# Cross-attention with two branches on one core: another order of VectorE's and ScalarE's work inside a batch

## The reference

```python
query = x @ Wq;  keyt = enc @ Wk;  valt = enc @ Wv
hs = mha(query, keyt, valt)                      # 100 queries, 718 keys, 8 heads
ca_q1 = einsum('btc,th->bch', ca, Wq_ca)[:, picked_100_rows, :]
ca_hs1 = mha(ca_q1, x, x)                        # second branch, 100 keys
ca_hs2 = mha(ca_hs1 @ Wq, ca @ Wk_ca, ca @ Wv_ca)   # 4 keys
out = (hs + ca_hs2) @ Wout + b_out + x
```

## Time and profile before

| | |
|---|---|
| runs | 995.15 us median (993.74 to 997.84) |
| the profiled execution | 995.7 us, its span 994.0 us, mean granted clock 0.995 |
| PE matmuls | 968.8 us busy, 97% |
| DVE | 709.8 us, 71% |
| ACT | 491.7 us, 49% |
| POOL | 343.2 us, 35% |
| DMA | 195 MB, mean 196 GB/s |

### The profile page before, as it was taken

One profiled execution on the slowest core, in us unless ns is written; L12 is line 12 of the kernel. 1 busy time (PEld: TensorE's weight loads), 2 busy tenths in 40 slices (PEclk: granted clock), 3 DMA queues, 4 the chain that ended last, 5 costly groups with the idle time before them and its releaser, 6 DMA issues.

```text
span 994.0 us, 21024 instructions
## 1 busy us (share of the span) xinstructions
PE 968.8 (97%) x6644; PEld 945.5 (95%) x6644; DVE 709.8 (71%) x1257; ACT 491.7 (49%) x911; POOL 343.2 (35%) x302
## 2 busy tenths in 40 slices
PE   9999899999999999999999999999999999998998
PEld 8998789999999999999999999999999999997997
DVE  6455677777777778787777777777777777777444
ACT  6434545455554546464646363636464645454120
POOL 5222253434242516060615252433333433424000
PEclk9999999999999999999999999999999999999999
DMA  7899967797878797979797868787888878795364
GB/s 260 278 287 269 273 155 191 184 206 182 196 184 200 182 190 189 191 191 190 198 182 197 188 194 194 193 180 202 181 213 163 226 162 218 164 223 149 101 188 142
DMA packets 157545, 195.21 MB, mean 196 GB/s; under 512 B 81040, under 2 KB 111568, under 8 KB 157520
## 3 DMA queue, kind: packets, MB, share of 16 engines
q1 hardware_dynamic: 150000, 181.53, 74.7%
q10 hardware_dynamic: 7520, 13.35, 4.4%
HBM read 82.74 MB, written 19.95 MB: 103 GB/s over the span
## 4 chain that ended last, share of the span: by engine, by line
PE 83%; DVE 8%; issue 3%; ACT 2%; SPq 1%; DMA 1%; ACTq 0%; DVEq 0%
PE psS L780 21%; PE psB L815 16%; PE psB L820 8%; PE psS L755 7%; PE psT L796 6%; PE psS L930 6%; PE psT L848 4%; PE psT L854 2%; PE psB L827 2%; PE psB L825 2%; DVE negmax L1580 1%; DVE probs L1591 1%; PE psB L965 1%; PE psB L880 1%; PE psB L903 1%
## 5 line engine op out<-in xcount | busy, mean ns | idle before, releaser
L780 PE MATMUL psS<-encT_keep,Wk_keep 128*128 128x360 f32 x1440 | 255.7, 331 | 1.8 <-ACT probs L1172 1.8
L780 PEld LDWEIGHTS psS<-encT_keep,Wk_keep 128*128 128x128 f32 x1440 | 239.2, 189 | 2.8 <-issue 1.4
L1172 ACT ACTIVATE probs<-psS,negmax 100x718 f32<-100x718 f32 x128 | 110.2, 861 | 137.1 <-DVE negmax L1580 137.1
L815 PE MATMUL psB<-PT_h,encN_h 128*128 128x400 f32 x480 | 169.3, 353 | 0.0
L815 PE MATMUL psB<-PT_l,encN_h 128*128 128x400 f32 x480 | 165.6, 345 | 0.0
L635 POOL TENSOR_TENSOR encT_keep<-encT_raw,encT_keep 128x718 fp32r<-128x718 f32 x45 | 83.5, 1856 | 181.7 <-ACT encT_keep L1201 177.2
L1597 DVE TENSOR_TENSOR PT_l<-psT,PT_h 128x600 fp32r<-128x600 f32 x128 | 99.5, 778 | 39.5 <-ACT PT_h L1183 36.0
L626 POOL TENSOR_TENSOR Mbd<-Mbd,fmask 128x320 fp32r<-128x320 f32 x48 | 43.1, 898 | 219.4 <-DMA Mbd<-m_split 216.8
L1580 DVE TENSOR_REDUCE negmax<-psS 100x1 f32<-100x720 f32 x128 | 114.8, 897 | 0.0
L1591 DVE TENSOR_SCALAR probs<-probs,inv 100x718 f32<-100x718 f32 x128 | 108.8, 850 | 4.5
L1183 ACT ACTIVATE PT_h<-psT 128x600 fp32r<-128x600 f32 x128 | 85.7, 669 | 44.6 <-PE psT L796 40.9
(11 more groups left out here) (253 smaller groups left out, 1793.5 us busy)
## 6 DMA issues: line engine op xcount, KB each, us to landing
kstack<-kT SPq DMA_DIRECT2D x64, 448.8 KB
kstack<-kT SPq DMA_DIRECT2D x192, 112.2 KB
enc_raw<-in_encN_dram SPq DMA_DIRECT2D x48, 384.0 KB, 4.4
encT_raw<-in_encT_dram SPq DMA_DIRECT2D x45, 359.0 KB, 5.2
kstack<-kT SPq DMA_DIRECT2D x32, 359.0 KB
kstack<-kT SPq DMA_DIRECT2D x32, 269.2 KB
kstack<-kT SPq DMA_DIRECT2D x32, 179.5 KB, 3.4
kstack<-kT SPq DMA_DIRECT2D x64, 89.8 KB, 3.8
```

The costliest lines, as they stand in the source:

```text
L780: mm = pe.matmul(keys_in(f, first)[:, half, 0:HALF], w[:, c, f * 128:(f + 1) * 128], e[:, c, k0:k0 + HALF], start=(j == 0), stop=(j == 3 * ...
L815: pe.matmul(psB[:, 1, 0:RH], eN[0][:, k, cc], PT[p][:, k, rows], start=(k == 0 and p == 0), stop=False)
L1172: nc.scalar.activation(halves(P[h % PRING][0:S, 0:KEYS]), without_overlap(psS[score_slot[h]], S), ACT.Exp, bias=negmax[:, h:h + 1], accum_ ...
```

## The change

Nothing is computed otherwise; calls move within ACT's and DVE's lists.

In batches 1 to 15 on DVE, `u_low(i-1, 2)` goes ahead of `b2_norm`. In every batch `xm_low` goes ahead of `norm(i, 5)`, and `norm(i, 6)` goes from ahead of `keys`' low part `k_low(i+1, 0)` to behind `rowmax(i, 7)`. In batch 0 `k_low(0, 3)` goes ahead of `norm(0, 1)`, `q_low(3, 2)` ahead of `norm(0, 3)`, `rowmax(0, 5)` and `xm_add` ahead of `pt_low(0, 3)`; on ACT `xm_copy` and `expo(0, 5)` go ahead of `pt_high(0, 3)` and the DMA issues of `store_q3(4)`, and `xm_high` ahead of `enc_high(0, 0)` and `store_q3(5)`. In the last batch ACT does `wo_high(2)` before `expo(15, 4)`, and `enc_high(15, 0)` with `enc_twice` ahead of `pt_high(15, 3)`.

```diff
@@ ACT, batch @@
                     if last:
                         wo_high(0)
                         wo_high(1)
+                        wo_high(2)
...
                     if last:
-                        wo_high(2)
-                    pt_high(i, 3)
-                    if first:
-                        store_q3(4)
-                    else:
                         enc_high(i, 0)
                         enc_twice(i)
-                    if last:
+                    if first:
+                        xm_copy(i)
+                        expo(i, 5)
+                    pt_high(i, 3)
+                    if first:
+                        store_q3(4)
+                    elif last:
                         enc_high(i, 1)
                         enc_high(i, 2)
-                    xm_copy(i)
-                    expo(i, 5)
+                    else:
+                        enc_high(i, 0)
+                        enc_twice(i)
+                    if not first:
+                        xm_copy(i)
+                        expo(i, 5)
                     if first:
                         q_high(3, 5)
+                        xm_high(i)
                         enc_high(i, 0, first)
                         enc_twice(i)
                         store_q3(5)
-                    xm_high(i)
+                    else:
+                        xm_high(i)
@@ DVE, batch @@
                     norm(i, 0)
+                    if not first:
+                        u_low(i - 1, 2)
                     b2_norm(i)
                     if not first:
-                        u_low(i - 1, 2)
-                    norm(i, 1)
+                        norm(i, 1)
                     k_low(i, 3)
+                    if first:
+                        norm(i, 1)
...
                     pt_low(i, 1)
+                    if first:
+                        q_low(3, 2)
                     norm(i, 3)
-                    if first:
-                        q_low(3, 2)
...
-                    pt_low(i, 3)
-                    rowmax(i, 5)
-                    xm_add(i)
+                    if first:
+                        rowmax(i, 5)
+                        xm_add(i)
+                        pt_low(i, 3)
+                    else:
+                        pt_low(i, 3)
+                        rowmax(i, 5)
+                        xm_add(i)
                     if first:
                         q_low(3, 5)
                     rowmax(i, 6)
-                    norm(i, 5)
                     xm_low(i)
                     if not first:
                         hs_add(i - 1, 1)
-                    norm(i, 6)
+                    norm(i, 5)
                     if last:
                         u_low(i, 0)
                     else:
...
                     rowmax(i, 7)
+                    norm(i, 6)
                     if not last:
                         u_low(i, 0)
```

More of the change, by code:

```diff
@@ L1397, in batch @@
                         store_q3(4)
+                    elif last:
+                        enc_high(i, 1)
+                        enc_high(i, 2)
                     else:
@@ L1400, in batch @@
                         enc_twice(i)
-                    if last:
-                        enc_high(i, 1)
-                        enc_high(i, 2)
-                    xm_copy(i)
-                    expo(i, 5)
+                    if not first:
+                        xm_copy(i)
+                        expo(i, 5)
                     if first:
                         q_high(3, 5)
+                        xm_high(i)
                         enc_high(i, 0, first)
@@ L1764, in batch @@
                     pt_low(i, 1)
-                    norm(i, 3)
                     if first:
                         q_low(3, 2)
+                    norm(i, 3)
                     if not first:
```

## The result

The changed kernel takes 988.56 us (median of 5 runs, 987.3 to 989.7) against 995.15 before, a ratio of 0.9927 with an interval of 0.9902 to 0.9951. It is faster, as forecast, and inside the range of 977 to 989, but the gain is 6.6 us by the medians and 7.3 by the ratio, which goes by all runs, where 15.1 were forecast. The profiled execution took 987.66 us, its span 986.0.

The account below looks back on a forecast made before the run. PE's matmuls were taken as the bound. Terms of 7.5 + 0 + 4.7 + 2.9 = 15.1 us, and 0.55 to reach the median, came off the profiled 995.7 us: 980.0 us, range 977 to 989.

Parts of the forecast that it names:

- Part 3: Batch 0: reordered DVE and ACT calls save net 3.1 us of waits plus 1.6 for the clock, 4.7 in all.
- Part 2: Loop: norm(i, 6) behind rowmax(i, 7) costs PE 0; bounds 0 to a loss of 1.7 us per batch.
- Part 1: Batches 1 to 15: u_low(i-1, 2) ahead of b2_norm ends PE's wait at values, 7.5 us off.
- Rival B: Loop gives only its bare waits, "issue" being the wait's own cost: 3.5 instead of 7.5 us, 984.0 us; chance 0.14.
- With both `norm`s out of the way: Batch 0: k_low(1, 0), pt_low(0, 4), c2_copy and rowmax(0, 7) come about 3 us earlier, removing waits of 1.08 and 0.71.
- rival D: Loop: DVE loses to POOL twice per batch at norm(i, 6), turn(i, 6) waits 1.7 us, 1004 us; chance 0.04.
- The 1.08 ahead of `keys(1, 0)`: Batch 0: expo(0, 5) ahead of pt_high and two DMA issues removes this PE wait of 1.08 us.
- the 1.6 for the clock: Batch 0: with waits less close together the clock stays up, saving 4.76 - 3.14 = 1.6 us.
- Part 4: Batch 15: waits of 1.27 and 1.66 us go, tile(0, 0) starts 2.9 us earlier; between 0 and 3.5.
- so they add: Whole kernel: the parts follow one another in time with PE the bound between, so their gains sum to 15.1 us.
- C: Batches 0 and 15 give little, 1.5 + 1.4 instead of 7.6 us: 984.7 us; chance 0.15.
- E: Loop: PE waits the same at b2_turn or keys(i, 4) behind DVE; only the ends give, 987.5 to 995; chance 0.07.

Follow-up runs that it names:

- again: The changed kernel run once more with no edit: 986.55 us, ratio 0.9916 to the kernel before.
- p3: The kernel before with only the change's moves in batch 0: 994.71 us, ratio 1.0001.
- before 2: A second trace of the unedited kernel before: its loop took 720.20 us, batch 0 60.32 us and batch 15 43.75 us.
- p1: The kernel before with only u_low(i-1, 2) ahead of b2_norm in batches 1 to 15: 987.79 us, ratio 0.9929.
- bsq: The kernel before with SP's loads of the next queries ahead of the lift of keys(i+1, 0) in the loop: 1002.18 us, ratio 1.0068.
- p1sq: As bsq, and with u_low(i-1, 2) ahead of b2_norm in batches 1 to 15: 987.57 us, ratio 0.9937 to the kernel before.
- p2: The kernel before with only norm(i, 6) behind rowmax(i, 7) and xm_low ahead of norm(i, 5), batches 1 to 14: 995.19 us, ratio 1.0010.
- p4: The kernel before with only the change's moves in batch 15: 989.19 us, ratio 0.9953.
- n2b: The changed kernel with norm(i, 6), norm(i, 5) and xm_low back in their old places in batches 1 to 14, second run: 984.44 us, ratio 0.9907.
- sq: The changed kernel with SP's loads of the next queries ahead of the lift of keys(i+1, 0) in the loop: 982.08 us, ratio 0.9886.
- vb: The changed kernel with norm(0, 6) moved to behind k_low(1, 0), ahead of pt_low(0, 4), in batch 0: 985.95 us, ratio 0.9921.
- qh: The changed kernel with ACT's copy q_high(3, 3) ahead of expo(0, 4) in batch 0: 986.76 us, ratio 0.9940.
- best15: Changed kernel with the alterations of n2b, sq, vb and qh, and the lift of keys(15, 3) ahead of store_hs(14, 0) and Wout's read: 983.30 us, 0.9887.

## Why the prediction was right and wrong

The time lies inside the range because the range was wide; of the 15.1 us forecast 6.6 to 8.4 came. The step that failed is Part 3, 4.7 us that the runs show as 0. With the 1 to 3 us that Part 2 costs it accounts for what is missing.

**Part 1, 7.5 us: right.** Alone 7.1 us, 5.2 to 8.8. The four traces with before's loop have 719.6 to 721.6 us, the undisturbed ones 713.1 to 713.4: 6.2 to 8.5. Rival B ("issue" is the wait's own price) is wrong: where before and its like show 0.15 us of "issue" the batch takes 51.28 us, and 50.93 without it, so 0.35 us go, more than the 0.15 + 0.17 counted. What the prediction did not ask is why the wait went from 0.15 to 1.1 us. The last instruction of `b2_norm` (L1635) takes 0.99 us in six of before's 14 batches and 1.08 to 1.56 in the other eight, where POOL's L626 runs beside it, and these eight are the ones in which PE waits for `u_low` by name.

**Part 2, 0: wrong in size, right in its rows.** "Cost for PE: 0" rested on DVE, POOL and ACT, and there it held: PE waited at no `turn` of the loop, though DVE lost to POOL in 4 of 14 batches of `again`. What it left out is the DMA engines: they are full from 43 to 51 us behind `keys` (0.98 to 1.00 busy in all kernels with the old place of the loads), and the step moved DVE's `k_low`, which sets when the copies start. The packets take about a tenth longer, by what path is open, and it costs 1 to 3 us.

**Part 3, 4.7 us: wrong, it is 0.** This is the step that failed. "With both `norm`s out of the way" counted `norm(0, 6)` where it left and not where it came to: ahead of `u_low(0, 0)` and `pt_low(0, 5)`, beside POOL, as rival D has it for the loop. Up to the start of `keys(1, 1)` the gain is there: it stands 45.71 us behind `keys(0, 3)` before and 42.04 with the change, 3.7 us against a net of 3.1. Behind it PE waits the 2.0 to 3.1 us shown above, and little or nothing is left. The seven traces with before's batch 0 take 60.8 us for it in the mean, the eight with the change's 61.0, and p3's runs say 0.

Two more numbers of the sum belonged to one trace. The 1.08 ahead of `keys(1, 0)` stands with 0.86 in before 2 and in none of the other five traces with before's batch 0; in before one of ACT's DMA issues ahead of `pt_high(0, 3)` took 1.70 us, its neighbours 0.3 to 0.8. And the 1.6 for the clock was chance, not the order's: with the last waits the same (0.65 to 0.69, 1.05 to 1.08 and 0.71 us), before, p1, bsq and p1sq show a fall at 130 to 137 us and before 2, p2 and p4 none; of the eight with the changed order three show one behind `keys(1, 1)` (changed, n2b, sq).

**Part 4, 2.9 us: right in which waits go, in part lucky in size.** Both waits went, and PE waits 1.53 us ahead of `tile(0, 0)` in p4 instead of 0.61, as said. That growth has to come off: in all PE's waits in batch 15 fell by 1.3 us only, and the other 1.5 of the 2.9 are the clock, for which this part had no term. It fell in batch 15 in all seven traces without Part 4 (before, before 2, p1, p2, p3, bsq, p1sq) and in two of the thirteen with it, the changed kernel and vb, both with a late copy of over 2 us there. In four more with it (again, n2b, qh, best15) it fell behind `tile(0, 0)`, and the rest of the program took 81.3 us instead of 79.8. In the changed kernel's trace that copy, which no step foresaw, ate the gain. Whether the clock gives more than 1.5 us in the runs is not shown: p4's 4.7 has an interval of 2.8 to 6.6.

**The sum.** The parts measured alone give 7.1 - 1.0 + 0 + 4.7 = 10.8 us; the change gives 7.3 and 8.4, less Part 2 10.4 and 9.2. The difference has the size of what late copies cost, and that the parts get into each other's way there is likely, but each of the four numbers is known to about 2 us only, so "so they add" is not refuted. Of the rivals, C (the ends give little) was true of batch 0 and false of batch 15. E's idea, that PE waits again at the next thing, was true, but the thing was a DMA copy and not DVE.

## What to carry to other kernels

When a moved instruction is costed, cost it where it arrives as well as where it leaves, in each written-out copy of the loop. Before a wait of PE on another engine is taken out, look at how full the DMA engines are in the stretches in which copies feed PE: the next bound may be a copy whose place in the queue has to move too. When a load is moved, ask which engine starts on its landing, and what runs beside it then: that made bsq slower by 6.8 us. And do not count a fall of the clock, or an odd wait, of one trace as a term; take a second trace first.
